# A four-layer transformer and stencil kernel: prologue norms on VectorE, end without GpSimd, expert weights at the loop's head, one ring as bias buffer and as staging for the second pass's weights

## The reference

```
L0: hid = gelu(x @ down_W.T + down_b);  hid = hid @ W_expert[d].T + b[d] + emb[d]   # d: an index per sequence
    x = layernorm(x + hid @ up_W.T + up_b) * ln_gamma + ln_beta
L1: scale, shift = split(silu(sin_emb(t)) @ W_ada + b_ada)
    x1 = layernorm(x) * (1 + scale) + shift
    q, k, v = x1 @ Wq + bq, ...;  s = q k' / sqrt(32) + bias, masked;  p = softmax(s)   # 16 heads
    x2 = x1 + (p @ v) @ Wo + bo
    h  = layernorm(x2) * g2 + beta2;  x3 = x2 + gelu2(h @ W1 + b1) @ W2 + b2
L2: r  = x3 + gelu(x3 @ Wi[e] + bi[e]) @ Wo[e] + bo[e];  f = layernorm(r) * gamma[e] + beta[e]
L3: df = -(d_rows(A0 f) + d_cols(A1 f)) + 0.5 (dd_rows(B0 f) + dd_cols(B1 f) + 2 d_rows d_cols(B2 f))
    out = relu(f + df * dt)           # differences with one-sided formulas at the borders
```

## Time and profile before

| | us |
|---|---|
| median of 3 runs | 2718.52 (2716.98 to 2720.34) |
| the profiled execution: own time, span | 2718.5, 2716.7 |
| first pass: prologue, to PE's first q product | 89.8 |
| first pass: loop, eight iterations | 1066 |
| between the passes, to PE's first down product at 1211.7 | 56 |
| second pass: loop | 1424 |
| the end, from 2636 us | 81 |
| PE busy 2471.0, DVE 2004.5, POOL 1211.4, ACT 1153.1 | of 2716.7 |

### The profile page before, as it was taken

How to read it: one execution, slowest core, us unless ns; L and a number is a source line. 1 busy time by engine, 2 the same in 40 slices (tenths; PEclk the granted TensorE clock), 3 DMA queues, 4 the chain that set the end, 5 groups by cost and what they waited for, 6 DMA issues and landing times.

```text
span 2716.7 us, 46503 instructions
## 1 busy us (share of the span) xinstructions
PE 2471.0 (91%) x14115; PEld 1215.3 (45%) x14203; DVE 2004.5 (74%) x3845; ACT 1153.1 (42%) x2197; POOL 1211.4 (45%) x1024
## 2 busy tenths in 40 slices
PE   3699999999999999939999999999999999999982
PEld 1354545454545454514444444444444444444430
DVE  5585858585767676777868778779687886786877
ACT  2475757585757575732323222223232232332221
POOL 3554646454646464625334253243342433333526
PEclk7899999999999999969999999999999999999996
DMA  3444444444545444353222222132222321332222
GB/s 130 149 145 154 141 156 149 158 153 143 163 139 163 138 156 145 103 199 132 86 86 89 97 94 93 58 132 86 92 89 89 103 97 66 111 112 78 89 70 73
DMA packets 155668, 319.38 MB, mean 118 GB/s; under 512 B 17714, under 2 KB 23474, under 8 KB 155458
## 3 DMA queue, kind: packets, MB, share of 16 engines
q1 hardware_dynamic: 145666, 299.13, 33.6%
q10 hardware_dynamic: 9792, 17.83, 1.8%
HBM read 298.85 MB, written 17.86 MB: 117 GB/s over the span
## 4 chain that ended last, share of the span: by engine, by line
PE 40%; issue 7%; DVE 4%; POOL 4%; ACT 1%; DMA 0%; SPq 0%; DVEq 0%; POOLq 0%; ACTq 0%
PE ffn_bank L1337 13%; PE ffn_bank L1339 13%; PE ffn_bank L1338 12%; PE ffn_bank L1330 2%; POOL prod L1258 1%; POOL f L1248 1%; POOL x L1276 1%; PE ffn_bank L1396 1%; PE ffn_bank L1346 1%; ACT g L1458 0%; DVE tmp L1539 0%; DVE g2T_hi L1630 0%; DVE tmp L1579 0%; DMA b<-in_b 0%; DVE g2T_lo L1631 0%
## 5 line engine op out<-in xcount | busy, mean ns | idle before, releaser
L946 DVE CUSTOM_DVE_ANT_0 tiles<-bank,bias 128x512 f32<-128x512 f32 x512 | 324.1, 687 | 139.9 <-PE bank L595 125.4
L760 ACT ACTIVATE tiles<-tiles,nmax 128x512 f32<-128x512 f32 x512 | 363.4, 713 | 56.5 <-DVE nmax L946 56.4
L495 POOL TENSOR_TENSOR bias<-bias,mask_add 128x1024 f32<-128x1024 f32 x128 | 272.0, 2135 | 223.9 <-DMA bias<-in_bias 214.4
L618 PE MATMUL bank<-ident,tiles 128*128 128x128 f32 x2048 | 306.3, 285 | 39.4 <-ACT v L726 17.7
L618 PEld LDWEIGHTS bank<-ident,tiles 128*128 128x128 f32 x2048 | 227.9, 143 | 198.7 <-issue 81.6
L1630 DVE CAST g2T_hi<-g 128x512 f16<-128x512 f32 x256 | 189.7, 741 | 156.5 <-ACT g L1458 151.6
L1631 DVE TENSOR_TENSOR g2T_lo<-g,g2T_hi 128x512 f16<-128x512 f32 x256 | 271.1, 1059 | 8.8
L1458 ACT ACTIVATE g<-ffn_bank,bi 128x512 f32<-128x512 f32 x128 | 88.0, 687 | 362.2 <-PE ffn_bank L1339 331.9
L1258 POOL TENSOR_TENSOR prod<-grid,f 128x512 f32<-128x512 f32 x108 | 166.8, 1570 | 129.4 <-DMA grid<-in_grids 123.3
L1269 POOL TENSOR_TENSOR prod<-grid,f 128x512 f32<-128x512 f32 x64 | 105.1, 1662 | 267.4 <-DVE tmp L1568 145.9
L746 ACT ACTIVATE pT<-bank 128x512 f32<-128x512 f32 x256 | 151.2, 591 | 168.0 <-PE bank L618 168.0
(11 more groups left out here) (256 smaller groups left out, 5105.5 us busy)
## 6 DMA issues: line engine op xcount, KB each, us to landing
bias<-in_bias SPq DMA_DIRECT2D x256, 512.0 KB, 4.0
raw<-in_W_l SPq DMA_DIRECT2D x128, 512.0 KB, 3.3
grid<-in_grids SPq DMA_DIRECT2D x172, 256.0 KB, 3.3
xin<-in_x SPq DMA_DIRECT2D x36, 256.0 KB, 4.0
x2n<-x_rows SPq DMA_DIRECT2D x9, 1024.0 KB, 6.9
out<-outt ACTq DMA_DIRECT2D x36, 256.0 KB, 2.0
x_rows<-tiles ACTq DMA_DIRECT2D x32, 256.0 KB, 3.0
l_rows<-in_rows SPq DMA_DIRECT2D x8, 768.0 KB, 4.4
```

The source lines that it names most:

```text
L495: pool.tensor_tensor(bias[:, n % NB, :, :], bias[:, n % NB, :, :], mask_add[:, u % T, :].unsqueeze(1).to_broadcast([P, 2, S]), ALU.add).th ...
L618: mm = pe.transpose(bank[:, t * P:(t + 1) * P], tiles[:, 4 * (u % NR) + i, t * P:(t + 1) * P], ident[:, :])
L760: act.activation(tile, tile, ACT.Exp, scale=-1.0, bias=nmax[:, u % 2, i:i + 1], accum_out=rsum[:, j, h:h + 1]).then_inc(prob_ready, 1)
L946: dve.tensor_tensor_reduce(tiles[:, 4 * (u % NR) + i, :], bank[:, :], bias[:, half % NB, i % 2, :], -1.0, 3.0e38, ALU.add, ALU.min, nmax[: ...
```

## The change

It has five parts. (1) First prologue: the six weights get a staging place each (parts of `tiles` and of `pT`), so no load waits; `vec_in` is waited for later; the two norms are made by DVE alone, with two fused instructions a tile in place of four on three engines; PE transposes the normed tiles one by one; Wv and Wo are split after x1T. (2) Attention loop: the next sequence's expert weights (five DVE instructions) move from slot 0 to the head of the loop, and their load ahead of the x loads; in slot 2 ACT empties the q bank ahead of its fourth exponential. (3) `bias` and the second pass's staging and work buffers are one tensor, `stage`, which lives through both passes; after its loop SP loads the first four weight pieces and x2 of sequence 0 into it. (4) Second prologue: W1's first half is split first, PE waits only for what it needs, DVE makes h2 alone, the ring has four places. (5) End: POOL has no part in it; five fp32 products by scaled identities make the column differences of the B1 and A1 terms on PE; the grids are loaded whole, early, over W1; DVE's products go over W2.

```
-ACT_AFTER = {0: 3, 1: 3, 3: 2, 5: 0, 6: 3, 9: 0, 10: 3, 13: 0, 17: 0}
+ACT_AFTER = {0: 3, 1: 3, 2: 3, 3: 2, 5: 0, 6: 3, 9: 0, 10: 3, 13: 0, 17: 0}
-DVE_L0 = {0: (("expert_weights",),), 5: (("stats0", 0), ("stats0", 1)), 6: (("stats0", 2), ("stats0", 3)),
+DVE_L0 = {5: (("stats0", 0), ("stats0", 1)), 6: (("stats0", 2), ("stats0", 3)),
...
+NS = 4
+def weight_pieces(a):
+    w1 = [(a["W1"][c * P:(c + 1) * P, half * 1024:(half + 1) * 1024], (c, half)) for half in range(2) for c in range(C)]
+    w2 = [(a["W2"][k * P:(k + 2) * P, :].rearrange("(k p) n -> p k n", p=P), k) for k in range(0, NF, 2)]
+    return w1[:C] + w2[:2] + w1[C:] + w2[2:]
...
             def load_weight(i):
-                if i >= 2:
-                    sp.wait_ge(weights_split, i - 1)
-                sp.dma_start(raw_view(i, hi), src).then_inc(raw_in[i % 2], 16)
+                sp.dma_start(raw_view(i, hi), src).then_inc(raw_in[i], 16)
...
                 sp.wait_ge(x1_hi, it * C + C)
                 sp.sem_inc(sp_carrier, 1)
+                load_expert(bass.ds(nxt, 1))
                 for t in range(T):
                     load_x(nxt, t)
-                load_expert(bass.ds(nxt, 1))
...
+            sp.wait_ge(scored, 1 + B * T * H)
+            for i, (src, _) in enumerate(weight_pieces(a)[:NS]):
+                sp.dma_start(staged(stage, i), src).then_inc(stage_in[i], 16)
+            sp.wait_ge(x2_out, 1 + 64)
+            sp.dma_start(stage[:, NS:NS + 2, :]..., x2_dram[0]...).then_inc(stage_in[NS], 16)
...
 (vector, first prologue)
+            def norm_first(which, t):
+                times, plus = ((ln_g[:, :], ln_b[:, :]), (ada[:, 0, :], ada[:, 1, :]))[which]
+                link(dve.scalar_tensor_tensor(out=xin[:, t, :], in0=xin[:, t, :], scalar=mv[:, t, 0:1], in1=times,
+                                              op0=ALU.subtract, op1=ALU.mult))
+                dve.scalar_tensor_tensor(out=xin[:, t, :], in0=xin[:, t, :], scalar=rstd[:, t:t + 1], in1=plus,
+                                         op0=ALU.mult, op1=ALU.add).then_inc((ln0_ready, x1_ready)[which], 1)
...
 (tensor, second pass)
-            pe.wait_ge(w_split, 2 * C)
-            pe.wait_ge(dmat_in, 32)
+                    if n in (0, NF // 2):
+                        pe.wait_ge(w_split, C if n == 0 else 2 * C + 2)
...
 (sync, after the second loop)
+            sp.wait_ge(x3T_split, B * C)
+            sp.wait_ge(sum_ready, 1 + B * T)
+            for g in (3, 1, 2, 4, 0):
+                sp.dma_start(last_grid[g], a["grids"][g]...).then_inc(last_grid_in[g], 16)
...
 (gpsimd, after the second loop)
-            add_beta3(pool, B)
-            for t in range(T):
-                alpha_products(pool, B, t)
-                beta_products(pool, B, t)
+            for dst, k in ((half_id, 0.5), (minus_half_id, -0.5), (minus_id, -1.0)):
+                pool.tensor_scalar(dst, ident[:, :], k, None, ALU.mult).then_inc(last_id_ready, 1)
...
 (tensor, after the second loop)
             for t in range(T):
-                pe.wait_ge(alpha_done, B * T + min(T, t + 2))
-                stencil(pe, psum[t], t, False).then_inc(full[t], 1)
+                pe.wait_ge(last_beta_ready, t + 1)
+                pa, pb, _ = last_views(t)[0]
+                terms = ((half_id, pb[:, 2:D + 2]), (half_id, pb[:, 0:D]), (half_id, pa[:, 0:D]),
+                         (minus_half_id, pa[:, 2:D + 2]), (minus_id, pb[:, 1:D + 1]))
+                for i, (w, x) in enumerate(terms):
+                    mm = pe.matmul(psum[t][:, :], w, x, start=i == 0, stop=False)
+                if t:
+                    last_stencil(t - 1)
+            last_stencil(T - 1)
...
 (vector, after the second loop: last_products(t), then t >= 2: one fused sum of tile t - 2)
-            for t in range(T + 1):
-                if t < T:
-                    alpha(link, B, t)
-                    beta(link, B, t)
-                if t:
-                    total(B, dt[:, B - 1:B], t - 1, psum[t - 1])
+                link(... x = (f - mean) * gamma);  link(... x = x * rstd + beta)
+                for g, dst in ((3, pb[:, 1:D + 1]), (1, pa[:, 1:D + 1]), (2, m2), (4, m1[:, 1:D + 1])):
+                    dve.wait_ge(last_grid_in[g], 16)
+                    ins = dve.tensor_tensor(dst, last_grid[g][:, t, :], x, ALU.mult)
+                ... seven operations on 128x2 edges, then last_beta_ready
+                ... m0 = grid0 * x;  w = m1[2:] - m1[:-2];  w = 0.5 * w - m0;  msp and vsp lo
```

More of the change, by code:

```diff
@@ L110 @@
            14: (("rstd", 1),)}
-PROLOGUE_DVE = [("g",), ("e",)] + [(name, t) for name in ("y", "stats0", "stats1") for t in range(T)]
 def attention_slots():
@@ L216, in attention_pass @@
         full = [sem(f"bank{i}_full") for i in range(8)]
-        raw_in = [sem(f"raw{i}_in") for i in range(2)]
+        raw_in = [sem(f"raw{i}_in") for i in range(6)]
         vec_in = sem("vec_in")
@@ L894, in _ @@
-            while todo:
-                weight_lo(todo.pop(0))
+            l0_part(link, None, ("expert_weights",))
+            weight_lo(2)
+            dve.wait_ge(vec_in, 16 * len(VECS))
+            link(dve.tensor_scalar(bq[:, :], bq[:, :], 1.0 / math.sqrt(HD), None, ALU.mult))
+            l0_part(link, None, ("g",))
+            weight_lo(3)
+            l0_part(link, None, ("e",))
+            for name in ("y", "stats0"):
+                for t in range(T):
+                    l0_part(link, None, (name, t))
@@ new lines, in _ @@
+            rstd_first(0)
+            for t in range(2):
+                norm_first(0, t)
+            for i in range(2):
+                dve.wait_ge(ada_full, i + 1)
+                dve.tensor_tensor(rows[:, i * D:(i + 1) * D], psum[6 + i][0:B, :], b_ada[:, i * D:(i + 1) * D],
+                                  ALU.add).then_inc(rows_ready, 1)
+            dve.wait_ge(rows_ready, 2)
+            dve.tensor_scalar(rows[:, 0:D], rows[:, 0:D], 1.0, None, ALU.add).then_inc(rows_ready, 1)
+            for t in range(2, T):
+                norm_first(0, t)
@@ L896, in _ @@
+            for t in range(T):
+                l0_part(link, None, ("stats1", t))
+            rstd_first(1)
+            dve.wait_ge(ada_in, 16)
+            for t in range(T):
+                norm_first(1, t)
             for c in range(C):
                 l0_part(link, None, ("x1T", c))
+            weight_lo(4)
+            weight_lo(5)
             before = links[0]
@@ L1069, in ffn_pass @@
         halo_in = sem("halo_in")
-        w_raw_in = [sem(f"w_raw{i}_in") for i in range(6)]
         w_hi = sem("w_hi")
@@ L1288, in _ @@
             pool.wait_ge(vec_in, 16 * len(COLS))
[L1289 to L1290 removed]
+            pool.wait_ge(h2_ready, T)
             for t in range(T):
[L1292 to L1295 removed]
+                move_x2(pool, x2_first, t)
             with pool.Fori(0, B) as it:
@@ L1329, in stencil, with last_views @@
             for i, (w, x) in enumerate(terms):
-                mm = pe.matmul(bank[:, :], w, x, start=(i == 0), stop=(i == len(terms) - 1))
+                mm = pe.matmul(bank[:, :], w, x, start=begins and i == 0, stop=(i == len(terms) - 1))
             return mm
+        def last_views(t):
+            v = last_prod[t % 2]
+            ext = [v[:, i * (D + 2):(i + 1) * (D + 2)] for i in range(3)]
+            plain = [v[:, 3 * (D + 2) + i * D:3 * (D + 2) + (i + 1) * D] for i in range(2)]
+            return ext, plain
         @block.tensor
@@ L1677, in four_layers @@
     x2 = nc.dram_tensor("x2_rows", (B, S, D), F32).ap()
-    attention_pass(nc, a, ada_rows, x2)
-    ffn_pass(nc, a, x2, out)
+    with ExitStack() as ctx:
+        stage = ctx.enter_context(nc.sbuf_tensor("stage", [P, 6, 2 * D], F32))
+        stage_in = [ctx.enter_context(nc.semaphore(f"stage{i}_in")) for i in range(NS + 1)]
+        attention_pass(nc, a, ada_rows, x2, stage, stage_in)
+        ffn_pass(nc, a, x2, out, stage, stage_in)
 def stencil_blocks():
```

328 lines of the change are left out of this document (179 added, 149 removed).

## The result

The changed kernel takes 2631.7 us (median of four runs, 2629.99 to 2633.66), the kernel before 2718.4 on the same chip: a ratio of 0.9682, with a 95% interval of 0.9670 to 0.9694. The forecast was 2633. The total was met to 1.3 us, but not each of its terms, and the difference is what this part is about. That it was met so closely is in part luck: the loop gave 7.2 us more than forecast, the first prologue 5.1 less and the passage between the passes 1.4 less, and these errors cancel. In what follows "x for y" means x where the other kernel, or the forecast, has y.

A forecast was written before the change was run, and what follows sets the result against it. PE bounds the two loops; prologue, passage and end are chains over DVE, POOL and ACT. Savings 27.6 (prologue) + 21.6 (attention loop) + 7 (passage) + 29.6 (end) = 85.8 from 2718.5 give 2632.7, said 2633; range 2615 to 2662.

The forecast's parts named there:

- It gets 1.3 longer ... and about 1.1 longer by the Wk split: First prologue, down to first root: 19.9 us chain grows by the gelu's table load and the Wk split, root at 35.2.
- The doubt about the fusing: Norms: fused operations cost DVE some 0.25 us a tile, 3 us, more than the pair replaced; POOL's absence pays.
- Together 2.7 an iteration: Attention loop: expert weights moved (1.6 us) plus q copy moved (1.1) save 21.6 us in eight iterations.
- the two waits of rows 4 whole, 30.0: Attention loop, upper bound: PE's waits for the v and q bank copies both vanish, 30.0 us.
- Rival A: Attention loop gives nothing back, since gaps may move to the next bank: 2654 us; chance 0.12.
- Rival D: Freed loops make PE busier and pull its clock down; 3.4% lower costs 85 us, the whole gain; chance 0.03.
- two pauses of 1.5: Between the passes: with four ring places, DVE's last twelve splits pause twice, 1.5 us each.
- near 25: Between the passes, a sign: PE's first up comes near 25 us after the first pass.
- its working (1185): Between the passes: PE's first up at 1185 us on the timeline for 1200.66.
- about 49: Between the passes, a sign: down comes about 49 us after the first pass.
- Rival B: End: PE's clock stays low after pauses, 2652 us if throughout, +5 if only each set starts low; chance 0.10.
- Rival C: Both prologues: transfers hold them and the ring of four is too short, saving 18 and 0, 2650 us; chance 0.10.

The follow-up runs named there:

- p1: Changed kernel with the prologue's Wq load behind the small vectors and the expert's row, and the Wq and Wk splits moved later: 2628.2 us.
- f1: Changed kernel with each of the prologue's eight normed tiles made by three VectorE operations instead of two fused ones: 2641.3 us.
- l4: l1 plus eight useless PE products in slot 1 of every iteration, right ahead of the wait for the v copy: 2645.8 us.
- l1: Changed kernel with VectorE's five expert-weight operations back behind slot 0's copies in each attention loop iteration, load left early: 2657.5 us.
- r2: Changed kernel with three more places for the second pass's weight pieces, seven instead of four: 2626.8 us.
- e1: Changed kernel with one of VectorE's five grid products of each of the last four tiles made by GpSimd: 2634.3 us.
- p2: Changed kernel with GpSimd's prologue adds of bo moved behind the last low part of x1T: 2631.9 us.
- r1: Changed kernel with GpSimd's four adds of b2 between the passes moved behind the last of sixteen weight pieces: 2630.2 us.

## Why the prediction was right in sum and wrong in two terms

Two terms missed by 5.1 and 7.2 us in opposite directions, so that the sum came out close is luck. Which chains and waits end earlier was right in every stage; that GpSimd's first adds slow the prologue, and that a wait of PE costs clock as well as time, was missing.

*First prologue, 27.6 forecast, 22.5 measured.* The failed part is "It gets 1.3 longer ... and about 1.1 longer by the Wk split": 19.9 us of one chain became 25.5, not 22.3. I let GpSimd slow only the second norm and forgot that its adds of up_b start with bo's landing, just when the gelu is ready (2.0 us on the split, 0.76 on the gelu and 0.7 on the scaling of bq between them; Wk's part cost 0.8 for 1.1; together the 3.2; p1 took 2.5 back). The root took 2.2 us as said. A fused pair is 1.58 us start to start and not 1.34: each of its operations is 0.75, and the second waits 0.16 for the first: 1 us for the first norm. Behind the second root, GpSimd's part was 2.3 us, forecast 2.5. Of the 5.1 us, 3.2 stand ahead of the first root, 0.6 between its start and the second statistics, 0.2 on these, 0.9 on the second root and norm and 0.2 behind it. The doubt about the fusing was about the pair that stays on VectorE; f1 shows that against three plain operations there the fused pair is the cheaper.

*Attention loop, 21.6 forecast, 28.8 measured.* The step that failed is "Together 2.7 an iteration", with its bound, "the two waits of rows 4 whole, 30.0". It priced a wait of PE by its length at most. The wait for v also pulled the clock down behind it: the loop before misses 11.9 us of clock, after 1.6, and the 0.99 of the earlier trace rows that I read as full was this. l4 gives that part of the cost back, 12 us, with the bank as late as in l1. The expert weights were worth 20.6 to 26.4 us for 12.8, the q copy 1.2 to 7.0 for 8.8; both together 28.8. Rival A is out by the loop's length. Rival D had the clock's direction the wrong way round: fewer gaps raised it.

*Between the passes, 7 forecast, 5.6 measured.* The mechanism is the forecast's (down waits for the pieces, the ring's reloads set them); "two pauses of 1.5" were six with 6.1 us. First up came 27.6 us after the last output product. The prediction's "near 25" is counted from the pass's end; its working (1185) is 28.9 after that product, so up was 1.3 early, while down came at 50.0 for "about 49". r2 shows it: with seven places the pauses are gone and down is 5.2 us earlier, although up is 1.8 later.

*Second loop.* 0.7 us, forecast nothing. The clock falls four times in it before and three times after; the instructions are the same.

*End, 29.6 forecast, 29.1 measured.* Each step held: 8.17 for 8.2 a tile, 33.4 for 33.3, 43.05 for 43. Rival B's low clock came for the first set only. e1 shows that work on GpSimd beside costs VectorE more than it takes over; it does not show how much of the 29.1 us is this.

*Rival C* was true in part: bo's landing held the gelu by 0.76 us, and the ring was short.

## What to carry to other kernels

Where PE waits a little once in an iteration, look at the granted clock of the next few microseconds before pricing the wait: here a wait of 2.2 us cost 2.6 to 3.3, and filling it with useless products gave back 12 us in eight iterations without shortening it. Before an operation of GpSimd or VectorE is moved, look for what of the other engine stands at the new place: of three such moves one gave back nearly all that it won (p2: 2.6 of 2.7 us), one a part (r1), and one lost (e1). Before a difference of a few us in a stage is explained, look how much the stage varies in runs that leave it alone. A total that is met says little about its terms; cut both traces at the same events and compare stage by stage.
